# Output projection's weights are centred and split on VectorE beside pairs 8 to 13, kept in DRAM as f16 pairs and loaded in the last pair

## What is computed

```python
x = x + layernorm(attn(layernorm(x)))
x = x + layernorm(ffn(layernorm(x)))
# attn: q, k, v = x @ w.T + b, per head of 64
scores = q @ k.T / 8                 # causal
probs = softmax(scores)
return (probs @ v) @ wo.T + bo       # output projection
```

## Time and profile before

| | |
|---|---|
| median of 3 runs | 2397.23 us |
| profiled execution, its own time | 2399.07 us |
| its span, first to last instruction | 2396.9 us |
| mean granted TensorE clock | 0.981 |
| busy: TensorE, weight loads, VectorE, ScalarE, GpSimd | 95%, 60%, 71%, 73%, 69% |
| DMA packets and bytes | 1372307, 445.33 MB |

### The profile page before, as it was taken

The page is one execution under the profiler, slowest core; times in us unless marked ns, Lnnn a source line. Parts: engine busy times, 40 slices in busy tenths (PEclk is TensorE's granted clock), DMA queues, the critical chain, the costliest instruction groups (busy, mean ns, idle before and its releaser), DMA issues. The chain is left out here.

```text
span 2396.9 us, 70748 instructions
## 1 busy us (share of the span) xinstructions
PE 2274.4 (95%) x28698; PEld 1449.8 (60%) x28698; DVE 1690.6 (71%) x4148; ACT 1746.3 (73%) x2380; POOL 1654.6 (69%) x1291
## 2 busy tenths in 40 slices
PE   7999999999999998899999999999999679999996
PEld 4566667675757665557575757575766445445453
DVE  7587777777777765566666666666776846777777
ACT  5577777877787776677777777777787846666665
POOL 3588888888888876778888888888898822222221
PEclk9999999999999999999999999999999879999998
DMA  6699999999999999999999999999999976666662
GB/s 205 129 190 204 197 213 204 203 203 208 209 202 196 211 198 194 199 200 193 179 194 178 191 183 185 181 186 185 185 195 202 224 165 153 168 153 172 149 168 80
DMA packets 1372307, 445.33 MB, mean 186 GB/s; under 512 B 1316784, under 2 KB 1349952, under 8 KB 1371984
## 3 DMA queue, kind: packets, MB, share of 16 engines
q1 hardware_dynamic: 1371984, 440.81, 98.8%
HBM read 67.95 MB, written 41.94 MB: 46 GB/s over the span
## 5 line engine op out<-in xcount | busy, mean ns | idle before, releaser
L1072 POOL TENSOR_TENSOR hl<-probs,hl 128x1024 f16<-128x1024 f32 x544 | 1169.2, 2156 | 161.2 <-ACT hl L921 160.4
L914 ACT ACTIVATE probs<-s_ps,exp_bias 128x1024 f32<-128x1024 f32 (+7 forms) x768 | 633.7, 854 | 289.7 <-DVE exp_bias L742 289.4
L737 DVE TENSOR_REDUCE neg_max<-s_ps 128x1 f32<-128x1024 f32 (+7 forms) x768 | 676.5, 905 | 152.9 <-PE s_ps L529 149.9
L921 ACT ACTIVATE hl<-probs 128x1024 f16<-128x1024 f32 x544 | 575.0, 1057 | 85.8 <-DMA pt<-hl 69.8
L552 PE MATMUL o_ps<-v,pt 128*128 128x65 f16 x4352 | 432.5, 193 | 46.3 <-DMA pt<-hl 42.5
L552 PEld LDWEIGHTS o_ps<-v,pt 128*128 128x128 f16 x4352 | 401.4, 97 | 74.8 <-DMA pt<-hl 30.4
L553 PE MATMUL o_ps<-v,pt 128*128 128x65 f16 x4352 | 432.9, 194 | 0.0
L529 PE MATMUL s_ps<-nat 64*128 64x512 f16 (+3 forms) x3840 | 410.1, 351 | 23.5 <-ACT probs L914 20.7
L554 PE MATMUL o_ps<-v,pt 128*128 128x65 f16 x4352 | 431.6, 193 | 0.0
L553 PEld LDWEIGHTS o_ps<-v,pt 128*128 128x128 f16 x4352 | 400.6, 97 | 19.2
L554 PEld LDWEIGHTS o_ps<-v,pt 128*128 128x128 f16 x4352 | 401.2, 98 | 0.0
(11 more groups left out here) (190 smaller groups left out, 3612.4 us busy)
## 6 DMA issues: line engine op xcount, KB each, us to landing
w_raw<-in_w_pairs SPq DMA_DIRECT2D x46, 576.0 KB, 5.1
o_scratch<-o_hl SPq DMA_DIRECT2D x64, 256.0 KB, 3.1
out<-result SPq DMA_DIRECT2D x31, 512.0 KB, 3.2
x_in<-in_x SPq DMA_DIRECT2D x27, 512.0 KB, 4.8
pt<-hl SPq DMA_TRANSPOSE x544, 5.4
xn_scratch<-xn SPq DMA_DIRECT2D x16, 512.0 KB, 3.7
xn<-in_x SPq DMA_DIRECT2D x11, 512.0 KB, 4.0
x_in_c<-in_x SPq DMA_DIRECT2D x10, 512.0 KB, 4.2
```

The costliest lines, as they stand in the source:

```text
L737: nc.vector.tensor_reduce(neg_max[:, step.round, acc, h:h + 1], s_ps[(n + h) % S_RING][:, first:end], AX_X, ALU.max, negate=True).then_inc ...
L914: last = nc.scalar.activation(probs_of(n)[:, cols], s_ps[n % S_RING][:, cols], ACT.Exp, bias=exp_bias[:, step.round, acc, h:h + 1], scale= ...
L921: nc.scalar.activation(hl_of(n, 0), probs_of(n), ACT.Copy).then_inc(p_hi_done, 1)
L1072: nc.gpsimd.tensor_tensor(hl_of(n, 1), probs_of(n), hl_of(n, 0), ALU.subtract).then_inc(p_lo_done, 1)
```

## The change

- The eight raw blocks are loaded one after the other into `x_in`, whose use for the second batch row's tiles ended in pair 6. The first is issued at step 0 of pair 8, each other one right behind the store of the block before it.
- Each block is worked on by VectorE alone, in four parts at four steps that `wo_places` picks out of steps 1, 5, 7, 8, 10, 12, 14 and 16 of pairs 8 to 13: part 0 sums the rows and scales the mean, part 1 centres and scales, part 2 makes the f16 copy in `xn`, part 3 subtracts. Block 0 has steps 5, 7, 8, 10 of pair 8; block 1 steps 14, 16 of pair 8 and 1, 5 of pair 9; block 2 steps 10, 12, 14, 16 of pair 9. Blocks 3 to 5 have the same steps two pairs later, blocks 6 and 7 those of blocks 0 and 1 four pairs later, so that the last part lies at step 5 of pair 13.
- SyncE stores the f16 pair (512 KB) in the new DRAM tensor `wo_scratch` at the start of the step behind part 3, behind a wait for it.
- In the last pair the stored pairs are loaded into `arena`, one block at each of steps 5 to 12, behind the step's two transposes. The raw loads, the sums, centrings, copies and subtractions of that pair are gone from all engines.
- TensorE waits for these eight loads ahead of the first output projection, in place of the subtractions.

```diff
-WO_BY_ACT = 4
-
-WO_LOW_EARLY = 4
+WO_SLOTS = [(p, i) for p in range(HALF_PAIRS, PAIRS - 2) for i in (1, 5, 7, 8, 10, 12, 14, 16)][1:]
+WO_GAP = 4
+
+
+def wo_places():
+    out, free = [], list(WO_SLOTS)
+    for k in range(KT):
+        out.append(free[:4])
+        last = out[-1][3]
+        free = [at for at in free if (at[0] - last[0]) * NSTEP + at[1] - last[1] >= WO_GAP]
+    return out
+
+
+WO_STEPS = wo_places()
+WO_LOAD_STEP = 5
...
-        wo_raw = ([nat[PAIRS % 2][:, k, :].bitcast(F32) for k in range(4)]
-                  + [v_left[:, k * 2 * D:(k + 1) * 2 * D].bitcast(F32) for k in range(2)] + [w_raw[:, 0:D]])
-        wo_raw.append(wo_raw[0])
-
+        w_pair = arena[:, 0:2 * KT * D].rearrange("p (l k n) -> p k l n", l=2, k=KT)
...
+            def load_wo(k):
+                sp.dma_start(x_in[:], fin["w_view"][k]).then_inc(wo_raw_loaded, 16)
+
             def body(p, kind):
                 for i in range(NSTEP):
+                    if (p, i) == (HALF_PAIRS, 0):
+                        load_wo(0)
+                    for k, at in enumerate(WO_STEPS):
+                        if at[3] == ((p, i - 1) if i else (p - 1, NSTEP - 1)):
+                            sp.wait_ge(wo_lo_done, k + 1)
+                            sp.dma_start(wo_scratch[k], xn[:]).then_inc(wo_stored, 16)
+                            if k + 1 < KT:
+                                load_wo(k + 1)
...
                     if kind == "last":
-                        for k in ([0, 1] if i == 0 else [i + 1] if i < KT - 2 else []):
-                            if k == 0:
-                                sp.wait_ge(s_done, NTASK * (PAIRS - 1))
-                            if k == 4:
-                                sp.wait_ge(pv_done, NTASK * (PAIRS - 1))
-                            if k == 6:
-                                sp.wait_ge(w_lo_done, 3 * PAIRS)
-                            sp.dma_start(wo_raw[k], fin["w_view"][k]).then_inc(wo_loaded[k], 16)
+                        if i == WO_LOAD_STEP:
+                            sp.wait_ge(unit_done, N_UNIT * PAIRS)
+                            sp.wait_ge(wo_stored, 16 * KT)
+                        if WO_LOAD_STEP <= i < WO_LOAD_STEP + KT:
+                            sp.dma_start(w_pair[:, i - WO_LOAD_STEP],
+                                         wo_scratch[i - WO_LOAD_STEP].rearrange("p (l n) -> p l n", l=2)).then_inc(wo_loaded, 16)
...
-                    if kind == "last" and i == KT:
-
-                        sp.wait_ge(wo_lo_done, 1)
-                        sp.dma_start(wo_raw[KT - 1], fin["w_view"][KT - 1]).then_inc(wo_loaded[KT - 1], 16)
...
             pe.wait_ge(exp_done, NTASK * PAIRS)
-            pe.wait_ge(wo_lo_done, WO_LOW_EARLY)
-            pe.wait_ge(wo_lo_late, KT - WO_LOW_EARLY)
+            pe.wait_ge(wo_loaded, 16 * KT)
             pe.wait_ge(fin["ot_loaded"][0], 16)
...
-            def center_wo(k):
-
-                raw, mean = wo_raw[k], wo_mean[:, k:k + 1]
-                if k >= WO_BY_ACT:
-                    dve.wait_ge(wo_loaded[k], 16)
+            def wo_part(k, part):
+                raw, mean = x_in[:], wo_mean[:, k:k + 1]
+                if part == 0:
+                    dve.wait_ge(wo_raw_loaded, 16 * (k + 1))
                     nc.vector.tensor_reduce(mean, raw, AX_X, ALU.add).then_inc(wo_sum_done, 1)
-                dve.wait_ge(wo_sum_done, k + 1)
-                nc.vector.tensor_scalar(mean, mean, 1.0 / D, None, ALU.mult).then_inc(wo_mean_done, 1)
-                dve.wait_ge(wo_mean_done, k + 1)
-                nc.vector.tensor_scalar(raw, raw, mean, W_SCALE, ALU.subtract, ALU.mult).then_inc(wo_centered, 1)
-
-            def wo_low(k):
-                dve.wait_ge(wo_hi_done, k + 1)
-                nc.vector.tensor_tensor(fin["w_lo"][:, k, :], wo_raw[k], fin["w_hi"][:, k, :], ALU.subtract).then_inc(
-                    wo_lo_late, 1)
+                    dve.wait_ge(wo_sum_done, k + 1)
+                    nc.vector.tensor_scalar(mean, mean, 1.0 / D, None, ALU.mult).then_inc(wo_mean_done, 1)
+                if part == 1:
+                    dve.wait_ge(wo_mean_done, k + 1)
+                    nc.vector.tensor_scalar(raw, raw, mean, W_SCALE, ALU.subtract, ALU.mult).then_inc(wo_centered, 1)
+                if part == 2:
+                    dve.wait_ge(wo_centered, k + 1)
+                    if k == 0:
+                        dve.wait_ge(xn_stored, 16 * LN_TILES)
+                    else:
+                        dve.wait_ge(wo_stored, 16 * k)
+                    nc.vector.tensor_copy(xn[:, 0:D], raw).then_inc(wo_hi_done, 1)
+                if part == 3:
+                    dve.wait_ge(wo_hi_done, k + 1)
+                    nc.vector.tensor_tensor(xn[:, D:2 * D], raw, xn[:, 0:D], ALU.subtract).then_inc(wo_lo_done, 1)
...
+                    for k, at in enumerate(WO_STEPS):
+                        if (p, i) in at:
+                            wo_part(k, at.index((p, i)))
...
-                        if 3 <= i < 3 + WO_BY_ACT:
-                            center_wo(i - 3)
-                        if i in (7, 8, 9, 11):
-                            center_wo({7: 4, 8: 5, 9: 6, 11: 7}[i])
...
-                        if 13 <= i < 13 + KT - WO_LOW_EARLY:
-                            wo_low(WO_LOW_EARLY + i - 13)
...
-            def wo_sum(k):
-
-                act.wait_ge(wo_loaded[k], 16)
-                nc.scalar.activation(xn[:, 0:D], wo_raw[k], ACT.Copy, accum_out=wo_mean[:, k:k + 1]).then_inc(wo_sum_done, 1)
-
-            def wo_high(k):
-                act.wait_ge(wo_centered, k + 1)
-                act.wait_ge(unit_done, N_UNIT * PAIRS)
-                nc.scalar.activation(fin["w_hi"][:, k, :], wo_raw[k], ACT.Copy).then_inc(wo_hi_done, 1)
...
-                    if kind == "last" and 2 <= i < 2 + WO_BY_ACT:
-                        wo_sum(i - 2)
-                    if kind == "last" and 6 <= i < 6 + KT:
-                        wo_high(i - 6)
...
-            def wo_low(k):
-                pool.wait_ge(wo_hi_done, k + 1)
-                nc.gpsimd.tensor_tensor(fin["w_lo"][:, k, :], wo_raw[k], fin["w_hi"][:, k, :], ALU.subtract).then_inc(
-                    wo_lo_done, 1)
...
+    wo_scratch = nc.dram_tensor("wo_scratch", (KT, P, 2 * D), F16, kind="Internal").ap()
```

More of the change, by code:

```diff
@@ L186, in units_ending, with attend_phase @@
     return [u for u, part, n in UNIT_AT[kind][i:i + 1] if part == n - 1] if i >= 0 else []
-def attend_phase(nc, x, w_pairs, mask_in, xn_scratch, o_scratch, arena, fin):
+def attend_phase(nc, x, w_pairs, mask_in, xn_scratch, wo_scratch, o_scratch, arena, fin):
     with ExitStack() as ctx:
@@ L288, in attend_phase @@
         rows_loaded = sem("rows_loaded")
-        wo_loaded = [sem(f"wo_loaded{k}") for k in range(KT)]
+        wo_raw_loaded = sem("wo_raw_loaded")
+        wo_stored = sem("wo_stored")
+        wo_loaded = sem("wo_loaded")
         fin_mean_done = sem("fin_mean_done")
@@ L297, in attend_phase @@
         wo_lo_done = sem("wo_lo_done")
-        wo_lo_late = sem("wo_lo_late")
         x_view = x.rearrange("(b t p) d -> b t p d", b=B, p=P)
-        v_left = v[PAIRS % 2][:].rearrange("p t l h f -> p (t l h f)")
-        wo_raw = ([nat[PAIRS % 2][:, k, :].bitcast(F32) for k in range(4)]
-                  + [v_left[:, k * 2 * D:(k + 1) * 2 * D].bitcast(F32) for k in range(2)] + [w_raw[:, 0:D]])
-        wo_raw.append(wo_raw[0])
+        w_pair = arena[:, 0:2 * KT * D].rearrange("p (l k n) -> p k l n", l=2, k=KT)
         pt_left = pt[:].rearrange("p b n -> p (b n)")
@@ L1118, in body @@
                         norm_scale(LN_TILES + tile)
-                    if kind == "last" and 6 <= i < 6 + WO_LOW_EARLY:
-                        wo_low(i - 6)
                 if kind == "last":
@@ L1774, in attention_ffn @@
         fin = finish_inputs(nc, ctx, x, o_scratch, w_o, b_o, ident, ffn_in, ffn_probe, ffn_mix, own, rank, center, slope)
-        attend_phase(nc, x, w_pairs, mask, xn_scratch, o_scratch, fin["arena"], fin)
+        attend_phase(nc, x, w_pairs, mask, xn_scratch, wo_scratch, o_scratch, fin["arena"], fin)
         finish_phase(nc, fin, out)
```

## The result

In the first comparison, 18 runs of each, the changed kernel took 2401.72 us (2397.24 to 2404.67) and the kernel before 2397.48 us (2394.96 to 2400.74): ratio 1.0016, 95% interval 1.0010 to 1.0023, or 2.4 to 5.5 us more. A second chip gave 2401.41 against 2396.90 us. The forecast was 2399.7 us, range 2392 to 2406, and a change of under 4.8 us was put as the likeliest case. The sign and the place were right, the size somewhat low.

A forecast was written before the change was run, and what follows sets the result against it. The prediction took SyncE's queue of transposes and loads to bound the last pair's later part. +2.2 us there and +0.3 in pairs 8 to 13 made +2.5 on 2397.23, so 2399.7 us, range 2392 to 2406.

The forecast's parts named there:

- The bound: Last pair from 1871.4 on: SyncE's queue with its DMAs sets the pace; relieving ScalarE, VectorE and GpSimd counts as nothing.
- The price of a load: SyncE's queue in the last pair: a 512 KB raw load costs 0.8 us (issue alone) to 1.8 us (with stretched transposes).
- The lead and the wait: Last pair: removed loads bring step 8 forward 7.3 us; two of them had lain in step 4's wait, 2.3 to 3.5 us.
- The net in the last pair: Last pair: 7.3 us gained, then six additional later loads give back 4.7 to 10.8 us; taken as +2.2 us.
- the lower price of 0.8: Last pair: a load costs its issue alone, 0.8 us, which would make the net there -2.6 us.
- Pairs 8 to 13: VectorE's four parts per block and SyncE's load and store: from nothing to 3.3 us, taken as +0.3 us.
- the second rival: Pairs 8 to 13: VectorE's parts make the maxima late, 3.3 us instead of 0.3; 2402.7, with locks 2405 us; chance 0.18.
- 1 (loads hide): Last pair after step 8: the six additional loads lie in queue gaps; 2390 to 2394, said 2391 us; chance 0.16.
- 3: End of last pair: the first output projection waits for the last load, 1 to 3 us more, 2402 us; chance 0.06.
- the cover at 2 us: End of last pair: step 12's load lands by 1942, ahead of the first output projection at 1944.40 plus the shift.
- 4 (nothing shifts): Last pair's queue: nothing shifts, as transposes' durations follow the transfers' total, which stays; 2397.5 us; chance 0.12.

The follow-up runs named there:

- kernel 1: The changed kernel without the eight loads of the stored weights in the last pair: 2391.65 us, ratio 0.9966 to the kernel before.
- kernel 5: The kernel before, raw loads kept, without the last pair's sums, centrings, copies and subtractions on the weights: 2398.26 us, ratio 0.9999.
- the second trace: Profiled execution of the changed kernel run once more, nothing altered, on the second chip: 2401.41 us, ratio 1.0014 to the kernel before.
- kernel 3: The changed kernel with blocks 0 and 1 loaded at step 0 of the last pair, the other six at steps 5 to 10: 2399.67 us, ratio 1.0000.
- kernel 4: The kernel before with the changed kernel's work of pairs 8 to 13 added, last pair as it was: 2399.66 us, ratio 0.9999.
- kernel 2: The changed kernel with the same eight loads at the same steps issued by ScalarE instead of SyncE: 2402.10 us, ratio 1.0012 to the kernel before.

## Why the prediction was right

**The bound.** The last pair is set by the queue of transposes with its loads, and the other engines' work in it is worth nothing: shown by kernel 1 and, within its interval of 5 us, by kernel 5.

**The price of a load.** Forecast 0.8 to 1.8 us; measured 1.3 and, with the second trace, (113.2 - 99.8) / 8 = 1.7, and 1.5 by the medians. The spread between executions is nearly half as wide as my two ends are apart. The six raw loads that were taken away come out alike: a lead of 6.6 us and a wait of 2.7 make (6.6 + 2.7) / 6 = 1.6 us each. So there is no sign that the stored pairs, which lie otherwise in DRAM and in `arena`, are dearer to load than raw blocks.

**The lead and the wait.** Forecast for step 6 -3.8 and for step 8 -7.3 us, with a gap before the second transpose of step 4. Measured -2.9, -6.6 (-6.5 in the second trace) and a gap of 2.7 us. The working itself gives 1878.45 - 1870.8 = 7.7 for step 8; what made it too large is that transposes in a row took 2.9 us and not 2.57. The two loads that had lain in this wait are what the net loss comes from; kernel 3 gives two loads that place back and by its median loses nothing. One detail was wrong. I took the product of step 2's second head for the one waited for; it is the first head's, five tasks back. In the kernel before this one was done some 0.4 us before the transpose started (1850.91), so that transpose did not wait for it at all: it simply followed the one before it. The wait could be up to 0.4 us shorter than I worked out, with no effect on the sum.

**The net in the last pair.** Forecast +2.2, measured +1.4 and +4.1 at the last landing, 2.8 in the mean. This is the term that was set somewhat low: I had weighed in the lower price of 0.8, which no run showed. By the forecast's own working, with the measured lead of 6.6, it is 6 x 1.5 - 6.6 = +2.4, and at 1.7 per load +3.6. The last product ended at 1946.9 where 1946.5 was forecast, and this closeness is luck: of the 2.9 us by which it came later, 1.6 had come up before pair 15 began, in the start of pair 8, pair 10 and pair 14.

**Pairs 8 to 13.** Forecast +0.3; pairs 9 to 12 took +0.4 and +1.1 in the changed kernel's two traces, +1.1 in kernel 4's, and +0.3 to +0.7 in the seven other traces that have this work: +0.5 in the mean. Pairs 8 and 13 took 114.8 and 110.6 before, and within 0.1 of that in the changed kernel's two traces. The durations of parts 1, 2 and 3 (centring, cast, subtraction), ns min/median/max and first and last start:

```profile
L800 DVE TENSOR_SCALAR x_in<-x_in,wo_mean x8: 743/755/2670, 1106.0 to 1616.7; 128x1024 f32<-128x1024 f32 x8
L807 DVE CAST xn<-x_in x8: 770/1458/1545, 1113.3 to 1633.0; 128x1024 f16<-128x1024 f32 x8
L810 DVE TENSOR_TENSOR xn<-x_in,xn x8: 1215/1326/2000, 1124.6 to 1660.3; 128x1024 f16<-128x1024 f32 x8
```

The cast, which no row showed, was taken at 1.5 and took 1.46 in the median; the subtraction was taken at 2.07 and took 1.33; the centring at its worst took 2.67, over the 2.1 us of a step's free time. What decides between 0.74 and 2.67 is which engine starts first. Here a subtraction of GpSimd and a centring of VectorE start together, GpSimd 0.01 us ahead, and the centring ends 0.55 us behind the subtraction:

```profile
1163.53 2.67 DVE L800 TENSOR_SCALAR x_in<-x_in,wo_mean 128x1024 f32<-128x1024 f32 x1
...
1163.52 2.13 POOL L1071 TENSOR_TENSOR hl<-probs,hl 128x1024 f16<-128x1024 f32 x1
```

and here the centring starts first, and the subtraction takes 2.57 instead of 2.13 us:

```profile
1332.39 0.75 DVE L800 TENSOR_SCALAR x_in<-x_in,wo_mean 128x1024 f32<-128x1024 f32 x1
...
1332.56 2.57 POOL L1071 TENSOR_TENSOR hl<-probs,hl 128x1024 f16<-128x1024 f32 x1
```

Of the eight centrings of this trace three are of the first kind (2.66 to 2.67 us), three of the second (0.75 to 0.76) and two have no GpSimd instruction beside them (0.74). These waits are real, as the second rival had it, and TensorE hardly feels them. TensorE's waits in these pairs are one for the exponentials, of the kind of the earlier trace rows, in the first trace,

```profile
PE s_ps L541 <- ACT probs L927: 0.2, 1, 0.2
```

and in the second trace also two for transposes, which I put down to the stores and raw loads in SyncE's queue; no run isolates that:

```profile
PE o_ps L564 <- DMA pt<-hl: 0.5, 2, 0.3
```

**The rivals.** 1 (loads hide) falls by kernel 1: the opposite sign. 2 (late maxima, 3.3 us) falls by kernel 4. 3 falls by the row of the first output projection, which waits for the transpose of `o_scratch` as before, and not for `wo_scratch`:

```profile
1947.31 0.59 PE L1223 MATMUL s_ps<-arena,w 128*128 128x512 f16 x1 [0.38 <-DMA w<-o_scratch]
```

The last of L485's loads was issued at 1934.97 and such a load lands after 3.9 to 5.3 us:

```profile
DMA to landing us min/median/max: 3.9/4.5/5.3
```

So it was there by 1940.3, with a cover of 7 us. I had the issue right (1934 to 1936) but took the cover at 2 us; this was too careful, but it moved nothing. 4 (nothing shifts) falls by the table of leads. One slip in the chances changed nothing: a quarter of the 0.72 that forecast and rivals 2 and 3 have together is 0.18, and 0.23 was written for "slower".

**What stays open.** 4.2 us were measured and 2.5 forecast. With +2.8 in the last pair and +0.5 in pairs 9 to 12, 3.3 us are named. The rest is pair 14 (99.5 before, 100.4 and 99.9 after) and the tail (453.0, then 453.5 and 452.3), where a single execution scatters by as much: pair 14 takes 99.0 to 101.9 us in the twelve traces. No run of mine splits these.

## What to carry to other kernels

When a stage is set by one in-order queue with full DMA engines behind it, count what goes through it, not what the other engines save: 512 KB cost 1.3 to 1.7 us, and the time stayed within 1 us by the medians when another engine issued all eight. Then look for where in the queue a transfer costs little: in a wait the queue has for another reason (here 2.7 us at step 4), and behind its last urgent entry. Moving five of eight loads there, with the store ahead of them, turned +4 us into -2.4 (0.2 to 4.6). Order what goes behind the urgent entry by who waits for it: a store left behind the late loads is a candidate for a wait later.

## What the runs showed of the hardware

- The time for which SyncE is busy issuing a DMA is not the price of issuing. Transposes of one size take 2.6 to 2.8 us each with no load among them (15.43 / 6 before, 25.30 / 9 in kernel 1), and 3.6 in kernel 2 with loads of another issuer beside them (21.64 / 6).
- The first transpose of step 4 took 2.22 us with no load ahead of it and 4.44 with two of 512 KB: 1.1 us for each, beside their issue of 0.9.
- The centring of 128x1024 fp32 on VectorE takes 0.74 us by itself and 2.67 when a GpSimd subtraction of 2.13 us starts together with it, a factor of 3.6 at one shape. Where the centring starts first it takes 0.75, and the subtraction 2.57 instead of 2.13.
- TensorE's granted clock in the second half of the last pair lies between 0.67 and 0.77 in the twelve traces, and its idle share there doesn't order it: 43% idle at 0.77 in kernel 1 and at 0.72 before, 44% at 0.67 in kernel 5, 49% at 0.74 in kernel 3. The last product ends 1.55 us behind the last landing in all twelve, so the clock doesn't show there.
